# Two per-pixel Gaussian blurs: half of the weight products move to GpSimd over a DMA spread, and the order of every engine is written anew

## The reference

```python
h = relu(einsum('bchw,co->bohw', x, w1) + b1)           # 16 -> 32 channels
ks = relu(einsum('bohw,o->bhw', h, w2[:, 0]) + b2[0]) * 20.0 + 1.0
sigma = ks / 3.0                                        # one per pixel
logits = -gauss_kernel / (2.0 * sigma[..., None, None] ** 2)   # 9 x 9 per pixel
wgt = exp(logits); wgt = wgt / sum(wgt)                 # over the 81 taps
low_freq = sum over u, v of x_padded[.., u:, v:] * wgt[.., u, v]
enhanced = x + low_freq
out = (enhanced - mean) / sqrt(var + 1e-5)              # over the image, per channel
```

## Time and profile before

| | |
|---|---|
| median of 3 runs | 514.49 us (514.17 to 518.37) |
| the profiled execution: time, span | 518.3 us, 516.5 us |
| TensorE busy | 431.7 us, 84% |
| VectorE busy | 374.6 us, 73% |
| ScalarE busy | 279.2 us, 54% |
| GpSimd busy | 57.2 us, 11% |
| mean granted TensorE clock | 0.931 of full |
| first blur, second blur (from the page's slices and the lines' first and last starts) | about 212 to 336 us, 381 to 508 us |

### The profile page before, as it was taken

The page is one execution under the profiler, slowest core; times in us unless marked ns, Lnnn a source line. Parts: engine busy times, 40 slices in busy tenths (PEclk is TensorE's granted clock), DMA queues, the critical chain, the costliest instruction groups (busy, mean ns, idle before and its releaser), DMA issues. The chain is left out here.

```text
span 516.5 us, 16761 instructions
## 1 busy us (share of the span) xinstructions
PE 431.7 (84%) x7248; PEld 311.4 (60%) x7248; DVE 374.6 (73%) x563; ACT 279.2 (54%) x382; POOL 57.2 (11%) x76
## 2 busy tenths in 40 slices
PE   4578998877999649689999998469978899999971
PEld 2277952224988512357777787357746687777860
DVE  2695486763888875488999999239525899999953
ACT  0655476663333200189888888211015888888753
POOL 3230002321000000310000120000030000000000
PEclk9968999997999959999999999869987999999986
DMA  8840000000000000000000000000000000000004
GB/s 189 173 171 1 2 1 0 1 0 1 3 3 1 3 0 0 0 2 4 3 4 1 0 2 4 3 1 1 0 0 1 3 4 3 3 0 1 3 4 162
DMA packets 8088, 9.79 MB, mean 19 GB/s; under 512 B 5391, under 2 KB 6752, under 8 KB 7904
## 3 DMA queue, kind: packets, MB, share of 16 engines
q1 hardware_dynamic: 7008, 8.60, 6.0%
q10 hardware_dynamic: 1024, 0.36, 0.4%
HBM read 6.85 MB, written 2.11 MB: 17 GB/s over the span
## 5 line engine op out<-in xcount | busy, mean ns | idle before, releaser
L1110 DVE TENSOR_TENSOR g_wgt<-g_exponents,ps 128x1024 f32<-128x1024 f32 x128 | 150.9, 1206 | 4.4 <-PE ps L955 4.3
L1054 ACT ACTIVATE g_wgt<-g_wgt 128x1024 f32<-128x1024 f32 x128 | 132.4, 1061 | 18.6 <-DVE g_wgt L1110 17.7
L955 PE MATMUL ps<-ident,g_scl 128*128 128x128 f32 x512 | 78.9, 283 | 4.5 <-DVE g_scl L1101 3.6
L970 PE MATMUL ps<-g_wgt,g_xt 128*32 128x64 f32 x4096 | 72.6, 223 | 7.5 <-issue 7.4
L970 PEld LDWEIGHTS ps<-g_wgt,g_xt 128*32 128x32 f32 x4096 | 62.0, 111 | 27.2 <-issue 24.1
L955 PEld LDWEIGHTS ps<-ident,g_scl 128*128 128x128 f32 x512 | 56.3, 139 | 16.0 <-DVE g_scl L1101 4.7
L1038 ACT ACTIVATE g_hid<-ps,vec 128x512 f32<-128x512 f32 x32 | 22.0, 688 | 64.5 <-PE ps L914 64.5
L469 PE MATMUL ps<-conv_img,projblk 128*32 128x512 f32 x256 | 35.4, 673 | 0.0
L1351 PE MATMUL ps<-high,wb 128*128 128x512 f32 x72 | 30.6, 426 | 5.3 <-DVE rest L1380 5.3
L526 ACT ACTIVATE biased<-ps,beta_o 128x512 f32<-128x512 f32 x32 | 23.5, 746 | 13.6 <-PE ps L469 13.5
L1061 ACT COPY g_num<-ps 128x512 f32<-128x512 f32 x32 | 18.5, 578 | 22.0 <-PE ps L970 22.0
(11 more groups left out here) (163 smaller groups left out, 688.8 us busy)
## 6 DMA issues: line engine op xcount, KB each, us to landing
x<-in_x SPq DMA_DIRECT2D x8, 256.0 KB, 6.9
x<-in_x SPq DMA_DIRECT2D x1, 2048.0 KB, 8.2
out<-g_result SPq DMA_DIRECT2D x4, 512.0 KB, 3.9
windows<-band SPq DMA_DIRECT2D x4, 256.0 KB, 4.9
c_weight<-in_c_weight SPq DMA_DIRECT2D x1, 576.0 KB, 3.8
g_w<-in_g_w SPq DMA_DIRECT2D x2, 128.0 KB, 2.6
onehot<-in_onehot ACTq DMA_DIRECT2D x1, 128.0 KB
g_gband<-in_g_gband SPq DMA_DIRECT2D x2, 64.0 KB, 2.8
```

Source lines behind the costliest of these rows:

```text
L955: tr = pe.transpose(ps[:, u % 4, P * k:P * k + P], spread(scl[s][:, k, u:u + 1], [P, P]), ident[:])
L970: mm = pe.matmul(ps[32 * j:32 * j + 32, O_BANK, 64 * cb:64 * cb + 64], xt[(s + t) % 2][:, cb, b, :], wgt[s][b][:, t, cb, :], start=(t == 0 ...
L1054: act.activation(w, w, ACT.Exp).then_inc(weight, 1)
L1110: dve.tensor_tensor(wgt[s][u][:], spread(gband[:].unsqueeze(2), shape), spread(s_in, shape), ALU.mult).then_inc(logit, 1)
```

## The change

- VectorE multiplies only images 0, 1, 4, 5 (`BY_DVE`); GpSimd multiplies 2, 3, 6, 7 (`BY_POOL`), in all rows but row 0, where VectorE still does all eight. GpSimd can't read PSUM, so its operand comes by DMA: 1/ks^2 is now computed before the turn, pixels along the free axis (`ks_sq` = (20 relu + 1)^2 by Square on ScalarE, `srow` by a 128x128 reciprocal on VectorE); SP stores it to DRAM in four DMAs and, when these have landed, reads it back in four DMAs of 256 KB, each a 2 KB line broadcast to 128 partitions (`s_wide`).
- `pe_spread` runs for VectorE's four images only (slots 0 to 3, one bank each).
- `act_weight` takes Exp over a pair of neighbouring images at a time: four instructions of 2048 elements, in the pairs' order 0, 1, 2, 3, so that those of VectorE and GpSimd alternate.
- The two hidden matmuls write two banks and follow one another with no wait; `act_xt` is one copy of 1024 elements; the copies of the blur's sums (`num`) move from ScalarE to VectorE.
- `pe_row`, `act_row`, `dve_row` are written anew. `dve_enhance` and `dve_stats` of row r-1 stand at the end of row r on VectorE, behind `dve_num(r, 0)`; the extra row that drained them (RB + 1) is gone.

The diff, cut to its core:

```diff
+    s_dram = nc.dram_tensor(f"{tag}_s_rows", (RB, B, BANK), F32, kind="Internal").ap()
+
+    BY_DVE, BY_POOL = (0, 1, 4, 5), (2, 3, 6, 7)
+    s_wide = [[sb(f"s_wide{s}{j}", [P, CB, BLK * BLK]) for j in range(len(BY_POOL))] for s in range(2)]
...
+    def slots(r):
+
+        return list(enumerate(range(B) if is0(r) else BY_DVE))
+
+    def by_slot(r, v):
+
+        return v + 1 if is0(r) else 4 * r + 5 + v
+
+    def weights_of(s, b):
+        return wgt[s][b // 2][:, b % 2]
...
+    def pe_ks_turn(pe, r, s):
+
+        pe.wait_ge(small, 3 * r + 2)
+        pe.transpose(ps[:, MLP_BANK, P:2 * P], srow[s][:], ident[:]).then_inc(ks_turned, 1)
...
+        if v == 0:
+            pe.wait_ge(small, 3 * r + 3)
+        if is0(r):
+            if v >= 4:
+                pe.wait_ge(logit, v - 3)
+        else:
+            pe.wait_ge(logit, 4 * r + 1 + v)
+        b = slots(r)[v][1]
         for k in range(4):
-            tr = pe.transpose(ps[:, u % 4, P * k:P * k + P], spread(scl[s][:, k, u:u + 1], [P, P]),
-                              ident[:])
+            tr = pe.transpose(ps[:, v % 4, P * k:P * k + P], spread(scl[s][:, k, b:b + 1], [P, P]), ident[:])
         tr.then_inc(scl_spread, 1)
...
+        if do.first:
+            for v in range(4, B):
+                pe_spread(pe, 0, 0, v)
+        if do.lag:
+            pe_blur(pe, r - 1, 1 - s, 1, 0)
+            pe_turn(pe, r - 1, 0)
+        if do.next:
+            pe_ks_turn(pe, r + 1, 1 - s)
+        if do.lag:
+            pe_blur(pe, r - 1, 1 - s, 1, 1)
+        if do.next:
+            pe_spread(pe, r + 1, 1 - s, 0)
+            pe_spread(pe, r + 1, 1 - s, 1)
+        if do.main:
+            pe_xt(pe, r + 1, 1 - s)
+        if do.lag:
+            pe_turn(pe, r - 1, 1)
+        if do.main:
+            pe_blur(pe, r, s, 0, 0)
+        if do.next:
+            pe_spread(pe, r + 1, 1 - s, 2)
+        if do.after_next:
+            pe_hidden(pe, r + 2)
+        if do.main:
+            pe_blur(pe, r, s, 0, 1)
+        if do.lag:
+            pe_low(pe, r - 1)
+        if do.next:
+            pe_spread(pe, r + 1, 1 - s, 3)
+        if do.after_next:
+            pe_ks(pe, r + 2)
...
+    def act_square(act, r):
+
+        act.wait_ge(small, 3 * r + 1)
+        act.activation(ks_sq[:], relu[:], ACT.Square, bias=one[:, 0:1], scale=20.0).then_inc(ks_squared, 1)
+
+    def act_xt(act, g, s):
+
+        act.wait_ge(xt_mm, g + 1)
         if not (isinstance(g, int) and g < 2):
             act.wait_ge(blurred, 2 * (g - 1))
-        act.copy(xt[s][:, 4 * k:4 * k + 4, :, 0:C],
-                 ps[:, (XT_BANK, MLP_BANK)[k], :].rearrange("p (k b m) -> p k b m", k=4, b=B)).then_inc(xt_out, 1)
+        act.copy(xt[s][:, :, :, 0:C], ps[:, XT_BANK:MLP_BANK + 1, :].rearrange("p h (k b m) -> p (h k) b m", k=4, b=B))\
+            .then_inc(xt_out, 1)
...
+        if is0(r):
+            act.wait_ge(logit, 2 * pair + 2)
+        elif pair % 2 == 0:
+            act.wait_ge(logit, by_slot(r, pair + 1))
+        else:
+            act.wait_ge(logit_p, 4 * r + pair - 5 + 2)
+        w = wgt[s][pair][:].rearrange("p b t k m -> p (b t k m)")
         act.activation(w, w, ACT.Exp).then_inc(weight, 1)
...
+    def act_row(act, r, s, do):
+        if do.next and not do.first:
+            act_square(act, r + 1)
+        if do.main:
+            act_weight(act, r, s, 0)
+        if do.next and do.first:
+            act_square(act, r + 1)
+        if do.main:
+            act_weight(act, r, s, 1)
+            act_xt(act, r + 1, 1 - s)
+            act_weight(act, r, s, 2)
+        if do.after_next:
+            act_hidden(act, r + 2)
+        if do.main:
+            act_weight(act, r, s, 3)
...
+    def dve_inverse(dve, r, s):
+
+        dve.wait_ge(ks_squared, r + 1)
+        if not (isinstance(r, int) and r < 3):
+            dve.wait_ge(s_stored, 64 * (r - 2))
+        dve.reciprocal(srow[s][:], ks_sq[:]).then_inc(small, 1)
...
+    def dve_num(dve, r, i):
+
+        dve.wait_ge(blurred, 2 * r + i + 1)
+        if not is0(r):
+            dve.wait_ge(num_turned, 2 * r + i - 1)
+        dve.tensor_copy(num[i][:], ps[:, O_BANK, :]).then_inc(num_out, 1)
...
+        if do.next:
+            dve_relu(dve, r + 1)
+        if do.main:
+            dve_logit(dve, r, s, 0)
+        if do.next:
+            dve_inverse(dve, r + 1, 1 - s)
+        if do.main:
+            dve_logit(dve, r, s, 1)
+        if do.next:
+            dve_scale(dve, r + 1, 1 - s)
+        dve_mix(dve, r - 1, 0)
+        dve_num(dve, r - 1, 1)
+        if do.main:
+            dve_logit(dve, r, s, 2)
+            dve_logit(dve, r, s, 3)
+        dve_mix(dve, r - 1, 1)
+        if do.main:
+            dve_num(dve, r, 0)
+        dve_enhance(dve, r - 1)
+        dve_stats(dve, r - 1)
...
+    def pool_logit(pool, r, s, j):
+
+        b = BY_POOL[j]
+        if j % 2 == 0:
+            pool.wait_ge(s_in[s][j // 2], 16 * r + 16 * s)
+        if not (isinstance(r, int) and r < 2):
+            pool.wait_ge(blurred, 2 * r + b // 4 - 3)
+        shape = [P, 2, CB, BLK * BLK]
+        pool.tensor_tensor(weights_of(s, b), spread(gband[:].unsqueeze(2), shape),
+                           spread(s_wide[s][j][:].unsqueeze(1), shape), ALU.mult).then_inc(logit_p, 1)
+
+    def pool_row(pool, r, s, do):
+        if do.main and not do.first:
+            for j in range(len(BY_POOL)):
+                pool_logit(pool, r, s, j)
+        if do.next:
+            pool_stage(pool, r + 2, s)
...
+            for r in range(1, RB):
+                sp.wait_ge(small, 3 * r + 2)
+                for k in range(4):
+                    sp.dma_start(s_dram[r, :, P * k:P * k + P], srow[r % 2][32 * k:32 * k + B, :]).then_inc(s_stored, 16)
+                sp.wait_ge(s_stored, 64 * r)
+                for j, b in enumerate(BY_POOL):
+                    if r >= 3:
+                        sp.wait_ge(logit_p, 4 * (r - 3) + j + 1)
+                    row = bass.AP(tensor=s_dram.tensor, offset=(r * B + b) * BANK, ap=[[0, P], [1, BANK]])
+                    sp.dma_start(s_wide[r % 2][j][:].rearrange("p k m -> p (k m)"), row).then_inc(s_in[r % 2][j // 2], 16)
```

More of the change, by code:

```diff
@@ L995, in pe_row @@
     def pe_row(pe, r, s, do):
[L997 to L1030, removed]
@@ new lines, in act_row, with dve_relu @@
+    def act_row(act, r, s, do):
[13 more added lines that the diff above has]
+            act_weight(act, r, s, 3)
+    def dve_relu(dve, r):
+        dve.wait_ge(ks_mm, r + 1)
+        if not is0(r):
+            dve.wait_ge(ks_squared, r)
+        dve.tensor_scalar(relu[:], ps[:, MLP_BANK, 0:P], vec[:, VEC[tag + "_b2"]:VEC[tag + "_b2"] + 1],
+                          0.0, ALU.add, ALU.max).then_inc(small, 1)
@@ L1136, in dve_row @@
     def dve_row(dve, r, s, do):
-        for u in range(B):
-            if do.main:
-                dve_logit(dve, r, s, u)
-            if u == 0 and do.lag2:
-                dve_enhance(dve, r - 2)
-            if u == 1 and do.lag2:
-                dve_stats(dve, r - 2)
-            if 1 < u < 5 and do.next:
-                dve_small(dve, r + 1, 1 - s, u - 2)
-                if u == 4:
-                    dve_small(dve, r + 1, 1 - s, 3)
-            if u == 2 and do.lag:
-                dve_mix(dve, r - 1, 0)
-            if u == 6 and do.lag:
-                dve_mix(dve, r - 1, 1)
+        if do.first:
+            dve_logit(dve, 0, 0, 0)
+            dve_logit(dve, 0, 0, 1)
+            dve_relu(dve, 1)
+            dve_logit(dve, 0, 0, 2)
+            dve_logit(dve, 0, 0, 3)
+            dve_inverse(dve, 1, 1)
+            dve_logit(dve, 0, 0, 4)
+            dve_scale(dve, 1, 1)
+            for v in range(5, B):
+                dve_logit(dve, 0, 0, v)
+            dve_num(dve, 0, 0)
+            return
@@ L1202, in _ @@
                 pool.memset(xt[s][:, :, :, C:C + 1], 1.0).then_inc(const_ready, 1)
-            stage(1, 1)
-            with pool.Fori(0, 3) as i:
-                for p in range(2):
-                    stage(2 * i + 2 + p, p)
-            stage(RB, 0)
+            pool_stage(pool, 1, 1)
+            pool.wait_ge(band_ready, 2)
+            rows_of(pool, pool_row)
             if to_clear is not None:
@@ L1214, in _ @@
                 pe.wait_ge(a, 16)
-            pe_hidden(pe, 0, 0)
-            pe_hidden(pe, 0, 1)
+            pe_hidden(pe, 0)
             pe_ks(pe, 0)
-            pe_xt(pe, 0, 0, 0)
-            pe_ks_turn(pe, 0)
-            pe_spread(pe, 0, 0, 0)
-            pe_spread(pe, 0, 0, 1)
-            pe_xt(pe, 0, 0, 1)
+            pe_ks_turn(pe, 0, 0)
+            for v in range(4):
+                pe_spread(pe, 0, 0, v)
+            pe_xt(pe, 0, 0)
+            pe_hidden(pe, 1)
+            pe_ks(pe, 1)
             pe.wait_ge(const_ready, 4)
@@ L1252, in _ @@
                 beside(dve)
-            for k in range(4):
-                dve_small(dve, 0, 0, k)
-            dve.wait_ge(band_ready, 1)
+            dve_relu(dve, 0)
+            dve_inverse(dve, 0, 0)
```

(2 more changed lines are left out.)

168 lines of the change are left out of this document (62 added, 106 removed).

## The result

The kernel after takes 559.70 us (median of 4 runs, 556.45 to 561.96) against 516.43 for the kernel before on the same chip: a ratio of 1.085, 95% interval 1.076 to 1.094. It is slower, by about 43 us. The profiled execution took 559.1 us with a span of 557.2 and a mean granted clock of 0.896; before it was 518.3, 516.5 and 0.931.

A forecast was written before the change was run, and what follows sets the result against it. TensorE bound the kernel before; after, a chain through TensorE, VectorE and ScalarE would. The 514.5 us median plus 26.8 for two blurs gave 541, plus 15.6 for the clock 557 us; 8-in-10 range 537 to 576.

The forecast's parts named there:

- The closed chain: Steady blur row: TensorE 4.34, VectorE 5.46, ScalarE 4.81, 0.15 back to TensorE, one after another; 14.8 us against 13.44.
- the seven steps: First blur product of row 0 to that of row 7, per blur: 99.7 us against 90.5, +9.2.
- The exponential of 2048: ScalarE's Exp over a pair of images in act_weight: estimated at 1.95 us, pitch 1.85 us.
- rival (d): ScalarE switches activation tables at each Square, 1.28 us a load: +30 us or more; 0.09 shared with GpSimd as bound.
- GpSimd and transfers at nothing: GpSimd's products (1.9 us each) and the DMA stores and loads finish before needed, 4.8 us of cover: cost nothing.
- rival (b): GpSimd becomes the bound, its product over 3.4 us; at 4 us about +44, 585 us; 0.09 shared with table switches.
- The clock in the rows: TensorE's 2.5 us waits lower its clock in the blurs' steady rows: 1.3 us over 12 rows, 15.6 us.
- The starts: Each blur's first matmul to row 0's first blur product: 22.7 us against 18.9, +3.8 per blur.
- the walk: Adding durations and handoffs step by step through a blur's start, from first matmul to row 0's blur: 22.7 us.
- The ends: End of each blur, from row 7's first product to the statistics: +0.4 us, as row 7 waits for its fourth pair.
- the untouched stages: Arrival at blur 1 and the stage between the blurs, which the change doesn't touch: forecast 0.

The follow-up runs named there:

- The control: The changed kernel run once more without any edit, beside the kernel before: 555.76 us, ratio 1.072.
- the filled kernel: Changed kernel with 16 identity transposes in TensorE's wait ahead of the first blur product of every row from row 1 on: 544.59 us, ratio 1.048.
- the run with small products: Changed kernel with GpSimd's products cut to one eighth from row 2 on, other weights left stale: 556.03 us, ratio 1.074.

## Why the forecast came out

It was right: 557 forecast, 559.7 measured, and the cause is the one that it named. The control took 555.8. By its steps:

- **The closed chain: right.** 14.8 us a row forecast; 14.72 to 15.04 measured where the clock is full. At full clock the seven steps are after's first, 13.82, and the filled kernel's other six, 86.0: together 99.8 us, where the prediction has 99.7. Its links: TensorE 443.14 to 447.64 = 4.5 (4.34 forecast), VectorE 447.64 to 453.01 = 5.4 (5.46), ScalarE and handoff 453.01 to 457.86 = 4.85 (4.81 + 0.15). Cutting the chain in one place took away most of the loss, and an edit beside it nothing in the rows.
- **The exponential of 2048: right.** 1.95 us by the line through two activations, 1.907 measured, pitch 1.8. No load of a table stands between Square (0.40 us) and Exp in the steady rows (the one load in the blurs, ahead of the first exponential of blur 2, is there before too), so rival (d) had no case.
- **GpSimd and transfers at nothing: right, with the product mis-sized.** 2.37 us in place of 1.9: the line through a 512-element and a 2048-element multiply, whose operands have other shapes, was a poor guide. The error changed nothing, as the run with small products shows. The estimate from the Trainium skill ("GPSIMD Engine Reference", "Elementwise — side-by-side cycle accounting", 4.5 us for 2048 elements, halved), 2.25, was nearer, and still 5% low. The row of rival (b) was priced well: with twice the work it is 20.2 us by the formula that the prediction used. Its total was not: six steps of 2.4 us more and a last one of 5.4 make 39.6 us for two blurs, not 44. VectorE's product is 1.202 us beside GpSimd's and 1.206 before, so GpSimd's products don't slow it. The Trainium skill ("SBUF — State Buffer", "Who interferes with whom") has it so for a VectorE instruction with at most one input in SBUF, outside the two-port modes, and the trace agrees.
- **The clock in the rows: right in mechanism, off in size.** 12 rows at 1.3 us were forecast, 15.6 us; over the 99.8 the profiled run had 3.3 and 8.6 us, 12.0 in all, from 7 of 14 steps at 1.4 to 2 us each, and the control 13.5, from 8. A wait of 1.9 to 2.4 us in each row makes the clock fall after some of the waits, not after each.
- **The starts: mis-sized.** +13.0 in place of +7.6 (+10.5 in the control). Nearly all of the miss is in blur 1: the walk gave 22.7 us for it and it took 27.0, while blur 2, which took 22.7 before and so was forecast at 26.5, took 27.6. The walk took every step at full clock, and the windows show 0.81 and 0.70. The timelines after show where the time went in blur 1: row 0's first four spreads (16 transposes) took 224.88 - 221.41 = 3.5 us, not 1.95, and `dve_relu(1)` began 17.2 us after the first hidden matmul, not 14.1.

Timelines after of the start of blur 1, TensorE and then VectorE:

```profile
221.41 3.68 PE L960 MATMUL ps<-ident,g_scl 128*128 128x128 f32 x16 [0.28 <-DVE g_scl L1105]
224.88 1.91 PE L945 MATMUL ps<-ident,g_tile 128*128 128x128 f32 x8
...
241.71 1.10 PE L974 MATMUL ps<-g_wgt,g_xt 128*32 128x64 f32 x64 [1.19 <-ACT g_xt L1055]
```

```profile
231.94 0.35 DVE L1091 TENSOR_SCALAR g_relu<-ps,vec 128x128 f32<-128x128 f32 x1 [6.96 <-PE ps L930]
```

- **The ends: mis-sized the other way.** +0.8 forecast, -4.7 measured. Blur 1's end was 15.0 us before because TensorE had two gaps of "issue" in it, which the kernel after doesn't have there. The timeline of before, TensorE, shows them:

```profile
325.06 0.75 PE L970 MATMUL ps<-g_wgt,g_xt 128*32 128x64 f32 x35 [1.57 <-issue]
...
330.41 0.77 PE L970 MATMUL ps<-g_wgt,g_xt 128*32 128x64 f32 x40 [1.91 <-issue]
```

The errors of starts (+5.4), ends (-5.5), steps (-3.5, the clock's part) and the untouched stages (+1.9) cancel to -1.7 us, 42.4 forecast and 40.7 profiled. Against the kernel before run beside it the control is 36.6 us slower, and the first comparison 43.3, so 42.4 agrees with them only as well as they agree with each other. The nearness of 557 owes something to luck, then; the +18.4 us of the chain doesn't.

Two things stay open: why the clock falls after one wait of 2.2 us and not after the next (the first step of a blur, behind a wait of 1.19 us, varies in the same way), and what makes the issue gaps.

## What to carry to other kernels

Freeing an engine by a seventh of its work is worth nothing until its order is walked: follow one steady iteration through every engine by the semaphores, and look for a ring in which each engine waits for the one before. Here the ring was closed by two products that stood behind a copy that waits, and moving these two lines turned a change of +7% into one of +1%, with the `xt` transposes and one wait in the start into -1.6%. A second cost rides on such a ring: its waits drop TensorE's clock, and a few matmuls of no use in the wait tell how much that is.

## What the hardware showed that was not expected

- GpSimd's 128x1024 product of a broadcast line and a broadcast pattern took 2372 ns and 2366 ns in two kernels, 456 ns at 128x128: 2.14 ns an element and some 0.18 us beside it, where the 2048-element multiply of the earlier trace rows costs 1.76 ns an element. So the two can't be put on one line; their operands have other shapes, and which part of that makes the difference no run here tells.
- Identity transposes were enough to hold the clock: 16 of them (1.91 us) in each wait gave 1.00 over 58.1 and 59.7 us, where such rows without them had 1.00 and 0.95 in the first profile after, and 0.95 and 0.92 in the control.
- TensorE stood still for 0.5 to 3.2 us in the middle of bursts of matmuls that wait for nothing that the profile shows, in the reordered kernels as in the one before. As rows get denser these gaps cost a part of what the order gains.
